# First attention of a decoder layer: q and k centered through their weights, v's output product taken from x directly, q's row factors applied at the residual addition

## The reference

```python
qkv = x @ Wqkv + bqkv
q, k, v = jnp.split(qkv, 3, axis=2)
q = q - q.mean(axis=2, keepdims=True)
k = k - k.mean(axis=2, keepdims=True)
q2 = q * q
k2 = k * k
q2 = q2 / (q2.sum(axis=2, keepdims=True) + EPS_SUM)
q2 = _l2norm(q2, axis=-1)
k2 = k2 / (k2.sum(axis=2, keepdims=True) + EPS_SUM)
k2 = _l2norm(k2, axis=-2)
kv = jnp.einsum('bnc,bnd->bcd', k2, v)
t2 = jnp.einsum('bnc,bcd->bnd', q2, kv) / math.sqrt(N)
return (v + t2) @ Wln + bln
```

## Time and profile before

| | us |
|---|---|
| median of 3 runs | 1859.47 (1855.1 to 1859.72) |
| profiled execution | 1852.38 |
| its span | 1850.7 |
| PE busy | 1636.9 (88%) |
| DVE busy | 1186.3 (64%) |
| ACT busy | 1054.2 (57%) |
| POOL busy | 520.9 (28%) |
| granted TensorE clock, mean | 0.953 |

### The profile page before, as it was taken

One profiled execution on the slowest core, in us unless ns is written; L12 is line 12 of the kernel. 1 busy time (PEld: TensorE's weight loads), 2 busy tenths in 40 slices (PEclk: granted clock), 3 DMA queues, 4 the chain that ended last, 5 costly groups with the idle time before them and its releaser, 6 DMA issues. The chain is left out here.

```text
span 1850.7 us, 35359 instructions
## 1 busy us (share of the span) xinstructions
PE 1636.9 (88%) x12288; PEld 1366.7 (74%) x12288; DVE 1186.3 (64%) x2778; ACT 1054.2 (57%) x2625; POOL 520.9 (28%) x449
## 2 busy tenths in 40 slices
PE   3878784999999999999999999985299999999995
PEld 3767673667767777676776777764199999999995
DVE  6888864665766757757577575562266666666662
ACT  2343422775775757757567476660066666666663
POOL 3343411000030120210302103012335555554544
PEclk8989987999999999999999999997599999999997
DMA  2112102101121031121211201046757877777783
GB/s 80 35 35 69 35 23 68 58 30 63 35 92 55 33 105 55 60 76 35 95 69 48 93 13 60 1 174 251 243 124 172 184 171 179 180 173 169 174 183 43
DMA packets 106111, 177.80 MB, mean 96 GB/s; under 512 B 13729, under 2 KB 51921, under 8 KB 105937
## 3 DMA queue, kind: packets, MB, share of 16 engines
q1 hardware_dynamic: 71120, 134.09, 22.6%
q0 software_dynamic: 28896, 38.62, 11.4%
q10 hardware_dynamic: 5920, 2.84, 0.7%
HBM read 107.27 MB, written 68.24 MB: 95 GB/s over the span
## 5 line engine op out<-in xcount | busy, mean ns | idle before, releaser
L1060 ACT ACTIVATE xa_prob<-xa_S,xa_nmax 128x512 f32<-128x512 f32 (+3 forms) x512 | 266.0, 535 | 141.8 <-DVE xa_nmax L1184 131.3
L1620 POOL DMA_INDIRECT out<-ex_y,ex_x x158 | 256.6, 1624 | 263.4 <-ACT ex_y L1569 140.2
L1523 PE MATMUL ex_H<-ex_xT,ex_w 128*128 128x256 f32 x1896 | 248.2, 288 | 7.6 <-DVE ex_xT L1589 7.6
L1523 PEld LDWEIGHTS ex_H<-ex_xT,ex_w 128*128 128x128 f32 x1896 | 234.1, 193 | 8.0 <-issue 8.0
L1537 PE MATMUL ex_Y<-experts_w_hi,ex_hT 128*128 x1264 | 234.2, 279 | 0.0
L1184 DVE TENSOR_REDUCE xa_nmax<-xa_S 128x2 f32<-128x1024 f32 (+3 forms) x256 | 198.0, 815 | 28.3 <-PE xa_S L921 20.1
L1423 POOL DMA_INDIRECT expert_rows<-xa_xn,xa_rows x128 | 124.6, 974 | 274.3 <-DVE xa_prob L1196 226.5
L1537 PEld LDWEIGHTS ex_Y<-experts_w_hi,ex_hT 128*128 128x128 f32 x1264 | 198.9, 188 | 0.0
L1595 DVE TENSOR_TENSOR ex_hT<-ex_h,ex_hT 128x512 fp32r<-128x512 f32 x158 | 109.6, 694 | 123.9 <-ACT ex_hT L1562 91.4
L1074 ACT ACTIVATE xa_probT<-xa_work 128x512 f32<-128x512 f32 x256 | 139.7, 604 | 71.4 <-PE xa_work L933 70.3
L1537 PE MATMUL ex_Y<-experts_w_lo,ex_hT 128*128 x632 | 176.8, 280 | 0.0
(11 more groups left out here) (252 smaller groups left out, 3381.0 us busy)
## 6 DMA issues: line engine op xcount, KB each, us to landing
ex_w_raw<-in_w SPq DMA_DIRECT2D x79, 512.0 KB
ex_x<-expert_rows SPq DMA_DIRECT2D x79, 273.0 KB
w_split<-xa_w_split SPq DMA_DIRECT2D x32, 512.0 KB, 2.8
xa_w_split<-in_w SPq DMA_DIRECT2D x32, 256.0 KB
experts_w_hi<-w_split SPq DMA_DIRECT2D x16, 512.0 KB
experts_w_lo<-w_split SPq DMA_DIRECT2D x16, 512.0 KB, 10.2
expert_rows<-xa_x SPq DMA_DIRECT2D x16, 273.0 KB
a_x<-in_x SPq DMA_DIRECT2D x8, 512.0 KB, 4.8
```

The lines of the kernel that those rows point to most:

```text
L1060: m = act.activation(prob[n % 2][:, odd, PROB_AT[i]:PROB_AT[i] + width], SB[slot[at]][:, odd, col:col + width], ACT.Exp, bias=nmax[n % 2][ ...
L1523: m = pe.matmul(bank[:, (f % 2) * ROWS:(f % 2 + 1) * ROWS], ww[:, c, f * P:(f + 1) * P], xx[:, c, :], start=(i == 0), stop=(i == len(terms ...
L1620: pool.indirect_dma_start(out, bass.IndirectOffsetOnAxis(x_in[j % NX][:, a, ID:ID + 1].bitcast(I32), 0), y[j % NY][:, a, :], None, compute ...
```

## The change

- The means of q and k vanish: the mean over the columns of each weight row is taken off Wq and Wk once, before they are split, and off their biases. Products then are q and k already centered. q's and k's bn_stats, aggregates and negated means go; the row sums of the squares are accumulated by ACT in the squaring itself.
- v's way to the output goes through one matrix: Wv Wln (and its bias) is made once in the preamble, from Wln and a transposed copy of Wv given as a further input. `Wall` holds q, k, v and this product, 1024 columns; a tile is two 128x512 products, "qk" and "vv". y is never formed. The right half of vv is v Wln with both biases; POOL adds x to it (`add_x`).
- The state is made transposed (v against k2), multiplied by Wln, and only then scaled by k's norms, while ACT and DVE take it from PSUM (`kvl`).
- q's squares are transposed unscaled; the row factor (`weigh_q`) is applied by DVE when it adds the product with `kvl` to the residual (`take_y`), row by row.
- k4 goes from POOL to ACT. v's low part and the residual's sum are now POOL's work at two places of a round.
- One order is written out for each engine instead of `plan`. Four PSUM banks are used in turn for qk, vv and y. x transposed is held once, not twice; the chunk has its own buffer; x is loaded when the residual sum of two batches before is done.

```diff
--- before.py
+++ after.py
...
+        turns = []
+        for b in range(B + 1):
+            turns += [(kind, b, t) for u in range(2) for kind in ("qk", "vv") for t in (2 * u, 2 * u + 1)] if b < B else []
+            turns += [("y", b - 1, u) for u in range(2)] if b >= 1 else []
+        turn_at = {key: i for i, key in enumerate(turns)}
+        bank_of = lambda key: work[turn_at[key] % 4]
...
-        plan = [("find_mean", 0), ("normalise", 0), ("residual", 0), ("transpose_x", 0), ("split_wln", 0)]
-        for b in range(B + 1):
-            projecting, attending, coming = b < B, b >= 1, b + 1 < B
-            plan += [("project", (b, 0))] * projecting + [("find_mean", b + 1)] * coming
-            plan += [("spread", (b, 0))] * projecting
-            plan += [("state", b - 1)] * attending + [("chunk", b - 1)] * (0 <= b - 1 < len(chunks))
-            plan += [("project", (b, 1)), ("spread", (b, 1))] * projecting + [("normalise", b + 1)] * coming
-            plan += [("square", (b, 0)), ("scale", (b, 0))] * projecting
-            plan += [("attend", b - 1)] * attending
-            plan += [("residual", b + 1), ("transpose_x", b + 1)] * coming
-            plan += [("square", (b, 1)), ("scale", (b, 1))] * projecting + [("output", b - 1)] * attending
+        chunk_of = lambda b: b - 1 if 1 <= b <= len(chunks) else None
...
+            load(0)
+            sp.dma_start(wln32[:], rows('Wln')).then_inc(wln_in.of("in"), 16)
+            sp.dma_start(wvT32[:], rows('WvT1')).then_inc(wvT_in.of("in"), 16)
+            sp.dma_start(bln[:], row_of(d['bln'], D)).then_inc(bln_in.of("in"), 16)
+            load(1)
+            for b in range(B + 1):
+                k = chunk_of(b)
+                if k is not None:
+                    name, c = chunks[k]
+                    w.wait_ge(chunk_lo, k - 1, k >= 1)
+                    sp.dma_start(chunk_in[:], d[name][c * P:(c + 1) * P, :]).then_inc(chunk_loaded.of(k), 16)
+                if b + 2 < B:
+                    w.wait_ge(x_norm, b)
+                    w.wait_ge(xb_ev, (b, 1))
+                    load(b + 2)
+                if b >= 1:
+                    w.wait_ge(work_ev, ("y", b - 1, 1))
+                    sp.dma_start(x1_dram[b - 1], x1[(b - 1) % 2][:]).then_inc(x1_stored[(b - 1) % 2].of(b - 1), 16)
...
+            def turn(key):
+                i = turn_at[key]
+                w.wait_ge(work_ev, turns[i - 4] if i >= 4 else None, i >= 4)
+                return bank_of(key)
...
+            def project(b, u):
+                w.wait_ge(xT_hi, (b, KC - 1))
+                w.wait_ge(xT_lo, (b, KC - 1))
+                w.wait_ge(w_lo, "qkv")
+                for kind in ("qk", "vv"):
+                    if kind == "vv":
+                        w.wait_ge(vl_hi, "weight")
+                        w.wait_ge(vl_lo, "weight")
+                    at = slice(0, 512) if kind == "qk" else slice(512, 1024)
+                    for t in (2 * u, 2 * u + 1):
+                        bank = turn((kind, b, t))
+                        for c in range(KC):
+                            for i, (a, ww) in enumerate(split3(xT, Wall)):
+                                m = pe.matmul(bank[:], a[:, c, t * P:(t + 1) * P], ww[:, c, at],
+                                              start=(c == 0 and i == 0), stop=(c == KC - 1 and i == 2))
+                        m.then_inc(work_pe.of((kind, b, t)), 1)
+
...
+            for c in range(KC):
+                for k in range(KC):
+                    for i, (a, ww) in enumerate(split3(WvT, Wln)):
+                        m = pe.matmul(KV[:, c * D:(c + 1) * D], a[:, k, c * P:(c + 1) * P], ww[:, k, :],
+                                      start=(k == 0 and i == 0), stop=(k == KC - 1 and i == 2))
+            m.then_inc(vl_pe.of("weight"), 1)
+            w.wait_ge(w_lo, "bvB")
+            for k in range(KC):
+                for i, (a, ww) in enumerate(split3(bvB, Wln)):
+                    m = pe.matmul(NB[:, 0:D], a[:, k, :], ww[:, k, :], start=(k == 0 and i == 0),
+                                  stop=(k == KC - 1 and i == 2))
+            m.then_inc(vl_bias.of("product"), 1)
...
+                            for i, (a, ww) in enumerate(split3(v[done % 2], k2s)):
+                                m = pe.matmul(KV[:, c * D:(c + 1) * D], a[:, t, c * P:(c + 1) * P], ww[:, t, :],
+                                              start=(t == 0 and i == 0), stop=(t == N_TILES - 1 and i == 2))
+                    m.then_inc(kv_pe.of(done), 1)
...
+                    w.wait_ge(kv_hi, done)
+                    w.wait_ge(kv_lo, done)
+                    w.wait_ge(kn_copy, done)
                     for c in range(KC):
+                        for k in range(KC):
+                            for i, (a, ww) in enumerate(split3(kvT, Wln)):
+                                m = pe.matmul((KV, NB)[c][:, 0:D], a[:, k, c * P:(c + 1) * P], ww[:, k, :],
+                                              start=(k == 0 and i == 0), stop=(k == KC - 1 and i == 2))
+                        m.then_inc(kvl_pe.of((done, c)), 1)
...
+                                for i, (a, ww) in enumerate(split3(sqT, kvl)):
...
+            def square(b, u):
+                w.wait_ge(sqT_pe, (b - 2, KC - 1), b >= 2)
+                w.wait_ge(qf_ev, b - 2, b >= 2)
+                w.wait_ge(k2_ev, (b - 1, u), b >= 1)
+                for t in (2 * u, 2 * u + 1):
+                    w.wait_ge(work_ev, ("qk", b, t))
+                    act.activation(sq_k[:, t, :], qk[:, t, D:512], ACT.Square, accum_out=s2[b % 2][:, t, 1:2]
+                                   ).then_inc(squared.of((b, t, "k")), 1)
+                    act.activation(sq_q[b % 2][:, t, :], qk[:, t, 0:D], ACT.Square, accum_out=s2[b % 2][:, t, 0:1]
+                                   ).then_inc(squared.of((b, t, "q")), 1)
+                    w.wait_ge(squared, (b, t, "q"))
+                    act.activation(sq4[:], sq_q[b % 2][:, t, :], ACT.Square, accum_out=s4[b % 2][:, t:t + 1]
+                                   ).then_inc(squared.of((b, t, "q4")), 1)
...
+            def fourth(b, u):
+                ts = slice(2 * u, 2 * u + 2)
+                w.wait_ge(k2_ev, (b, u))
+                w.wait_ge(nb_pe, b - 1, b >= 1)
+                act.activation(k4[:, ts, :], k2[:, ts, :], ACT.Square).then_inc(k4_ev.of((b, u)), 1)
...
+                    act.activation(Wall[0][:, c, js], stage[:, c, js], ACT.Identity, bias=w_mean[:, c, j:j + 1])
...
+            def take_vv(b, t):
+                w.wait_ge(vl_bias, "sum")
+                w.wait_ge(v_hi, (b - 1, t // 2), b >= 1)
+                w.wait_ge(v_lo, (b - 1, t // 2), b >= 1)
+                w.wait_ge(xb_ev, (b - 1, t // 2), b >= 1)
+                w.wait_ge(work_pe, ("vv", b, t))
+                dve.tensor_tensor(vv[:, t, :], bank_of(("vv", b, t))[:], bias[:, 512:1024], op=add
+                                  ).then_inc(work_ev.of(("vv", b, t)), 1)
...
+            def scale_k(b, u):
+                ts = slice(2 * u, 2 * u + 2)
+                inv = s2[b % 2]
+                w.wait_ge(squared, (b, 2 * u + 1, "q4"))
+                dve.tensor_scalar(inv[:, ts, :], inv[:, ts, :], EPS_SUM, None, add).then_inc(s2_eps.of((b, u)), 1)
+                w.wait_ge(s2_eps, (b, u))
+                dve.reciprocal(inv[:, ts, :], inv[:, ts, :]).then_inc(s2_inv.of((b, u)), 1)
+                w.wait_ge(s2_inv, (b, u))
+                w.wait_ge(k2_hi, (b - 1, u), b >= 1)
+                w.wait_ge(k2_lo, (b - 1, u), b >= 1)
+                w.wait_ge(k4_ev, (b - 1, u), b >= 1)
+                for t in (2 * u, 2 * u + 1):
+                    i = dve.tensor_scalar(k2[:, t, :], sq_k[:, t, :], inv[:, t, 1:2], None, mult)
+                i.then_inc(k2_ev.of((b, u)), 1)
...
+            def weigh_q(b):
+                r, aq = s4[b % 2], s2[b % 2][:, :, 0]
+                w.wait_ge(s4_root, b)
+                w.wait_ge(s2_inv, (b, 1))
+                dve.tensor_tensor(r[:], r[:], aq, op=mult).then_inc(s4_a.of(b), 1)
+                w.wait_ge(s4_a, b)
+                dve.tensor_scalar(r[:], r[:], EPS_NORM, float(S) ** 0.5, ALU.max, mult).then_inc(s4_b.of(b), 1)
+                w.wait_ge(s4_b, b)
+                dve.reciprocal(r[:], r[:]).then_inc(s4_c.of(b), 1)
+                w.wait_ge(s4_c, b)
+                w.wait_ge(work_ev, ("y", b - 1, 1) if b >= 1 else None, b >= 1)
+                dve.tensor_tensor(qf[:], r[:], aq, op=mult).then_inc(qf_ev.of(b), 1)
+
+            def take_y(b, u):
+                w.wait_ge(xb_ev, (b, u))
+                w.wait_ge(qf_ev, b)
+                w.wait_ge(x1_stored[b % 2], b - 2, b >= 2)
+                w.wait_ge(work_pe, ("y", b, u))
+                for t in (2 * u, 2 * u + 1):
+                    i = dve.scalar_tensor_tensor(x1[b % 2][:, t, :], bank_of(("y", b, u))[:, (t % 2) * D:(t % 2 + 1) * D],
+                                                 qf[:, t:t + 1], xb[b % 2][:, t, :], op0=mult, op1=add)
```

(73 more changed lines are left out.)

646 lines of the change are left out of this document (250 added, 396 removed).

## The result

| | before | after |
|---|---|---|
| median (range) | 1857.97 us (1855.1 to 1859.72, 4 runs) | 1791.2 us (1785.37 to 1793.32, 4 runs) |
| profiled execution / span | 1852.38 / 1850.7 | 1789.64 / 1787.6 |
| PE busy | 88% | 90% |
| DVE busy | 1186.3 us | 1141.9 us |
| granted clock, mean | 0.953 | 0.963 |

The ratio of the medians is 0.9637, 95% interval 0.9609 to 0.9665: faster by 3.6%. The forecast was 1797 us with a range of 1778 to 1823, so its sign and its range held, and its point but for 6 us. Between the two profiled executions the difference is 62.7 us against a forecast of 63; the medians differ by 66.8. What lies behind the first attention kept its length, as forecast: 1564.9 us before (from 285.83, where the next stage begins), 1565.2 after (from 222.41).

A forecast was written before the change was run, and what follows sets the result against it. DVE, in its fixed order, was taken to carry the round, PE paying in idle time and lower clock. First attention: 20.0 + 17 + 6 x 24.5 + 21.5 + 14 = 219.5 against 282.8, 63 us less: 1797 us, range 1778 to 1823.

The forecast's parts named there:

- preamble: Before the first q,k product: weight reductions, splits, transposes and new-weight products; 20.0 us, no change, bounds 18.5 to 23.
- round 0: First attention's first round: next x normalised at about 12, its transposed parts behind tile 3's squares; 17 instead of 22.5 us.
- round 7: First attention's last round, without a weight chunk and without a next x; 21.5 us.
- tail to the last eviction: After round 7: transposes, state, norms, Wln product, root and kvl, y, last eviction; 14 instead of 18.6 us.
- The second round's slip: DVE 3 to 4 us into the next round, ACT's squares slip about 1.5; second round 24.2, 24.5 with hand-overs.
- The check by DVE's sum: DVE's operations and stands in a round added up: 19.3 + 2.3 + 1.5 + about 1 = 24 us.
- The gap in front of y: PE's idle time before the y product in a round: 1.3 to 2.3 us, clock taken as kept.
- PE binds: Rival: in the rounds DVE's stands vanish in its slack; round 22.2 us, 1783 us in all; chance 0.19.
- The gap grows and the clock falls: Rival: gap before y over 3 us, y slow; round 27.7 us, 1816 us in all; chance 0.20.
- The work returns as waits: Rival: work taken from DVE returns as waits in the rounds; round 30 to 31 us, 1833 in all; chance 0.06.
- The clock never comes back: Rival: PE stands every round and never regains its clock; at f = 0.75 round 36.5, 1868 us; chance 0.03.
- it doesn't do what it says: Rival: q's factor or k's chain stays on the path, nothing gained; within 0.3% of 1859.5 us; chance 0.02.

The follow-up runs named there:

- the late chunk: Changed kernel with POOL's low part of the weight chunk moved behind the root of q's factor; 0.9619 of the kernel before, stage end 213.97 us.
- the kernel with the statistics put back: Changed kernel with the eight bn_stats of q and k per round back on DVE, results unused; 0.971 of the kernel before, stage end 233.83 us.
- order alone: Kernel before with only attend of batch b - 1 put ahead of scale of (b, 0) on every engine; 1.0053 of the kernel before, stage end 295.55 us.
- the last one: Changed kernel with POOL's chunk later, Wln product earlier, matmuls filling round 0's idle time, ACT's copy of v's weights earlier; 1782.61 us, 0.959 of the kernel before.

## Why the prediction was right, and where it was not

The stage's last eviction ended at 219.3 us against a forecast of 219.5. By parts:

| part | forecast | measured |
|---|---|---|
| preamble | 20.0 | 20.3 |
| round 0 | 17 | 18.2 |
| rounds 1 to 6 | 147 | 142.7 |
| round 7 | 21.5 | 22.5 |
| tail to the last eviction | 14 | 15.6 |
| sum | 219.5 | 219.3 |

**The sum is better than its terms.** 4.3 us too much in the rounds cancel 4.1 too little around them. That the sum is right within 0.2 us is luck; the mechanism is not.

**What binds a round.** Right, and shown: PE's list of 22.0 is measured at 22.0, and becomes the round (22.3) when the maximum no longer stands. The forecast's layout of a first such round had y start at 20.3 behind the round's start; in round 5 it is 155.16 - 134.81 = 20.35. Its marks at 14.1 to 16.5 for the maximum are 14.3 to 16.6 in the trace.

**The second round's slip.** Wrong: it took the first 3 to 4 us of DVE's backlog to push ACT's squares by 1.5 and so the whole round to 24.2. The backlog is there (3.1 us), but DVE's evictions of the first half have caught up with PE (in round 6 DVE waits 0.23 and 0.62 us for PE's vv products, at 162.57 and 163.88), and the steady round stays at 23.1 to 23.2, below the "24 to 25" that were to show the forecast. With the few tenths for hand-overs this is the mis-sized term, 1.3 a round, 8 us. Against it stand two terms that the forecast left out: round 1's slow start, 2.2 us, and DVE's scaling of two chunks, 0.6 each. The granted clock of 0.91 in round 1 is below the "above 0.95" of the forecast. The check by DVE's sum, which also gave 24, was no second proof: DVE is busy 21.6 of 23.1.

**The gap in front of y.** 1.11 to 1.76 in the six rounds, 1.3 to 2.3 forecast; it keeps the clock, as taken. Its releaser is ACT's high part of `kvl` and not DVE's low one, as said. The forecast drew the right chain (tile 3, squares, high parts), and named its last link.

**DVE.** 21.6 a round against "22 to 24". Its `scalar_tensor_tensor` of 256 columns, priced at 0.42 between 0.35 and 0.70, come at 0.43 and 0.48.

**Round 7 and the tail.** Round 7 was 1.0 over: ACT and DVE take `kvl` for 1.32 us with PE idle, since the transposes of a next x, which lie over it in the other rounds, are missing there; the 21.5 had no room for it. In the tail the same 1.28 us stood in the forecast as "root and kvl 1.5". What failed there are two other steps. PE did not wait "about 2 for DVE's last k split": the state starts at 204.83, 0.3 behind the transposes. And the clock fell, during the product with Wln (0.28 at 210.21, 0.41 at 210.91): that product took 2.5 instead of 1.4 and y 4.5 instead of 2.8.

**Round 0.** 1.2 over: the x transposes are split by ACT only behind the squares of two tiles (33.8 to 36.5), whose evictions wait in DVE's list behind k's scaling, which stood 0.7 us under POOL, and behind the normalisation of x, which waited 0.66 for POOL's root.

**The preamble** came out right for a partly wrong reason: ACT's table load of 1.28 us, which lay under the weights' load before, was on the path, so the products for the new weight began at 17.18 and not at 15.8; they took 3.1 instead of 3.9, as the clock rose among them (0.41 at 18.82, 0.28 at 19.37).

**The rivals.** *PE binds* did not hold, and the late chunk shows its price: it was put at 14 us for six rounds, and 6.8 is what the move brings there, since the round without it was 23.2 and not 24.5. *The gap grows and the clock falls* is what the kernel with the statistics put back does in three of its six rounds (gaps of 2.78, 3.40 and 2.79). *The work returns as waits* did not hold in this kernel, but it does with order alone in the kernel before (1.0053). *The clock never comes back* and *it doesn't do what it says* found nothing: 1.00 in rounds 2, 6 and 7.

## What to carry to other kernels

Lay out each engine's list for one round with measured durations before you count work: here the layout gave the gap, its place and its cause within half a microsecond, while the estimate of how delays add up from round to round was the part that failed. Look at what POOL does right after it releases a tiny DVE operation; moving a 2.4 us POOL item one place down was worth as much as eight statistics a round. And when a removed stall has a neighbour, ask what the stalled operation will meet next: idle time moved by order alone came back elsewhere, and 0.5% of the time was lost with it.

## What the runs showed of the hardware that was not expected

- A DVE operation of 0.17 us that is released by POOL's result lost to POOL's next queued operation each time: in rounds 1 to 6 it stands for the whole 2.4 us. One place later in POOL's list it takes 0.17.
- Not every POOL operation makes DVE stand. Under POOL's root of four columns (144.56, 1.03 us) k's scaling of two 128x256 took its usual 0.61; under the sum of 512 columns (157.27, 1.29 us) the same took 1.39.
- Nor does every DVE operation stand. The reciprocal of four columns, in SBUF, took its usual 0.18 at 157.37, under that same sum, between a tensor_scalar of four columns (1.16 at 156.17) and k's scaling (1.39), which both stood; so it was in every kernel that came from the changed one.
- Idle gaps of PE in front of y and the clock: 1.11 to 1.78, 1.89, 2.11, 2.15, 2.16, 2.30, 2.33, 2.53 and 2.91 us left it up; 1.84, 2.78, 2.79, 2.83 and 3.40 brought it down. The length alone doesn't decide. And the fall came up to 1 us behind the gap, in a stream already running again at full clock, as at 1.84 and 2.79.
- Hundredths of a microsecond can decide who stands: 0.03 us ahead, DVE's scaling took 0.68 and POOL stood for 0.5; 0.08 us behind, it took 1.75. An edit some 75 us earlier turned the one into the other.
- With two waits ahead of the first activation ACT's table load came behind both (at 8.24 us), with a single one ahead of it (at 1.34 in the kernel before and 2.40 in the last one).
